# The last batch of the first stage in a three-stage transformer kernel: one POOL operation moved up between its scatters, a table of counts moved behind them, and four experts' weights requested later

## The chip, the cores and the metric

One core of one Trainium2 chip runs the whole program. The engines are PE (matrix products), DVE (vector), ACT (activations), POOL (elementwise sums here, and the issue of indirect transfers), and SP, which only issues transfers. The metric is the device time of one execution in microseconds.

## The reference, cut to what matters

The input is `[8, 512, 256]` in float32. Four layers follow each other, each on the layer-normed stream, each added to it: attention with hyperbolic distances (16 heads of 16), a mixture of experts, attention with a low-rank latent, and a switch-head attention. The change lies where the first layer ends and the experts begin:

```python
logits = x.astype(jnp.float32) @ router_w.T          # 4096 tokens, 64 experts
topk_w, topk_ids = jax.lax.top_k(softmax(logits), K) # K = 8
pos = cumsum(onehot(flat_e), axis=0)[...] - 1        # place of a token among those of its expert
idx = where(pos < C, flat_e * C + pos, E * C)        # C = 128 slots for each of E = 64 experts
xb = zeros(...).at[idx].set(x[tok])                  # a token's row goes to its slots
h = silu(xb @ w_gate) * (xb @ w_up); y = h @ w_down  # w_gate, w_up [256, 192], w_down [192, 256]
routed = segment_sum(y[idx] * weight, tok)
shared = silu(sg) * su @ ws_down                     # two products for every token
```

An expert's weights in float32 are 256 x 384 and 192 x 256 elements, 384 KB and 192 KB (as 128 KB and 64 KB), 576 KB together.

## The kernel before, in words

The kernel has three stages, each a block with a barrier of all engines at its end. Stage one takes the 8 batches (B = 8, 512 tokens each) through the first attention and the routing. Its loop runs over rounds b = -1 to 9, and within each over 8 phases p, one for each pair of heads. Each engine has its own `cycle` function, called once for each (b, p), and the engines meet at semaphores alone. Work that isn't attention is spread over phases by hand-written tables. A batch's routing is done a round after its attention, so round b = 8 has no attention left: only the routing of the last batch, and whatever of the batch before it is open.

A batch's routing ends in a list, slot to token. For batches 0 to 6 POOL writes it: `scatter` issues 32 indirect transfers, each of which writes 128 token numbers of 4 bytes into a table in HBM at slots computed by DVE (`IDX`). In rounds 2 to 7 four of these go into each phase (SCATTERS = 4). Those of batch 6 are all issued in round 8, phase 0, behind the last head sums of batch 7 (`add_root`, L1049). Batch 7's own slots don't go through HBM: DVE makes matrices of marks (`mark`, L884 to L895), PE multiplies them (`list_last`), and DVE adds the result to the list that came back from HBM (`earlier`, L902) into `ids`. The marks need two small tables of counts, which POOL makes with two `iota` (L1074, L1075); a drain and the semaphore `counted` follow, and `mark` waits for it before its first operation.

The chain of the last batch in round 8: the last head group is placed, PE multiplies by `wo` (`output`, two products, each followed by a sum on DVE, L785), DVE takes mean and variance (`stats2`, semaphore `var2`), POOL raises it to the power -0.5 (`rsqrt`, L1042, at phase 4, so behind all that POOL does in phase 0), DVE normalises (`norm2`, L608), PE transposes (`turn2`, L384) and multiplies by the router's weights (`logits`), DVE takes the top 8 (`logits`, `slots`), then gate/up of the shared expert (`gate_up`), the router's weights (`weights`), `hid`, PE's last products and DVE's last sums (`shared`, L942), and SP stores the batch (L319). PE fills idle time with products that nobody reads (`keep_clock`, L365).

SP's order in round 8 is: at phase 3, once all of the attention's products are done, the weights of the first SOON = 4 experts (`request`, three transfers each, L196 to L198); at phase 5 the store of the normalised rows (L327), a wait for all scatters (L331), the load of the list (L332), and the weights of experts 4 to 11 (UN = 12 fit into the buffer); at phase 7 the store of the router's weights (L349); in round 9 the last store of the stream. All of these share one queue; POOL's indirect transfers have their own.

Stage two takes the 64 experts one by one. POOL waits for `ids`, gathers eight experts' rows ahead, then for each expert adds the result to the stream and gathers one more. SP requests expert e's weights when expert e - 12 is done. Stage three is the second attention pair.

## Time and profile before

| | us |
|---|---|
| three timed runs | 2812.64, 2803.64, 2807.13 |
| their median | 2807.13 |
| the profiled execution, its own time | 2811.8 |
| its span in the trace | 2810.1 |

Times in the rows count from the span's start. PE is busy 83% of the span, DVE 68%, ACT 60%, POOL 66%. Stage one lasts to about 1342.5 us, stage two to about 1570. A timeline row gives start, duration, engine, line, operation, output and inputs, and in brackets how long the engine was idle before it and what ended that; "issue" means that the profile shows nothing that it waited for. An engine name with a q is its sequencer, or for SP its queue of transfers.

### The profile page before, as it was taken

What the parts mean: (1) busy time and instruction counts of PE and PEld (TensorE: products, weight loads), DVE (VectorE), ACT (ScalarE), POOL (GpSimd) and SP (SyncE); (2) the same over time, 40 slices, a digit from 0 to 9 for tenths busy, and PEclk for the clock granted to TensorE, in tenths of its full rate; (3) what the DMA queues carried; (4) which work ended last, traced back from release to release, by engine and by line L of the source; (5) the groups of instructions that cost most, each with busy time, mean ns of one, the idle gap of its engine ahead of it and who ended that gap; (6) DMA issues with size and microseconds to landing.
All of it is one profiled execution on the core that took longest, in us unless ns stands there. A gap on an engine that the chain in (4) does not pass through costs nothing. (4 is left out here: it accounts for less than half of the span.)

```text
span 2810.1 us, 31463 instructions
## 1 busy us (share of the span) xinstructions
PE 2339.5 (83%) x10169; PEld 1174.3 (42%) x10169; DVE 1902.4 (68%) x3134; ACT 1673.5 (60%) x2352; POOL 1862.9 (66%) x1858
## 2 busy tenths in 40 slices
PE   5667777787777777775888799999999999999985
PEld 2222323232323323233555455555555555555543
DVE  5787989898988988763333356565756666666655
ACT  1778888889788888980122255555555555555440
POOL 0555587787878787873577302958585858595866
PEclk8667787878778787786899899999999999999997
DMA  3000000000000010114799500000000000000000
GB/s 104 16 1 1 17 16 16 18 16 18 9 25 8 10 23 3 30 15 107 218 265 226 112 1 1 1 1 23 1 23 1 23 1 20 4 8 1 9 0 16
DMA packets 94052, 98.97 MB, mean 35 GB/s; under 512 B 18848, under 2 KB 90656, under 8 KB 93856
## 3 DMA queue, kind: packets, MB, share of 16 engines
q1 hardware_dynamic: 70704, 73.99, 9.1%
q0 software_dynamic: 23152, 22.68, 4.6%
q8 instruction: 84, 1.38, 0.2%
q14 instruction: 112, 0.92, 0.2%
HBM read 69.98 MB, written 26.66 MB: 34 GB/s over the span
## 5 line engine op out<-in xcount | busy, mean ns | idle before, releaser
L1049 POOL TENSOR_TENSOR TT<-TT,SS 128x512 f32<-128x512 f32 x512 | 652.0, 1309 | 223.8 <-ACT SS L978 223.3
L1791 ACT ACTIVATE PR<-S,NM 128x512 f32<-128x512 f32 x512 | 345.3, 686 | 260.2 <-DVE NM L1958 260.2
L1958 DVE TENSOR_REDUCE NM<-S 128x2 f32<-128x1024 f32 x256 | 301.7, 1220 | 131.7 <-PE S L1685 131.7
L734 DVE TENSOR_SCALAR TT<-SC 128x1024 f32<-128x1024 f32 x256 | 311.6, 1217 | 75.4 <-POOL TT L1049 44.6
L464 PE MATMUL OB<-TT,VAL 128*17 128x512 f32 x1024 | 345.3, 777 | 4.6 <-ACT TT L986 4.6
L736 DVE SCALAR_TENSOR_TENSOR SS<-SC,TT 128x1024 f32<-128x1024 f32 x256 | 313.6, 1225 | 20.6 <-issue 1.8
L1054 POOL DMA_INDIRECT slot_tokens<-TID,IDX x224 | 229.3, 1024 | 101.1 <-issue 67.1
L1696 PE MATMUL TP<-ident,PR 128*128 128x128 f32 x2048 | 273.3, 276 | 21.2 <-DVE TT L1963 18.2
L1696 PEld LDWEIGHTS TP<-ident,PR 128*128 128x128 f32 x2048 | 235.0, 142 | 113.7 <-issue 66.9
L1963 DVE COPY TT<-TP 128x512 f32<-128x512 f32 x256 | 176.3, 689 | 151.4 <-PE TP L1696 147.6
L1797 ACT ACTIVATE TT<-TP 128x512 f32<-128x512 f32 x256 | 153.3, 599 | 195.1 <-PE TP L1696 191.3
L1715 PE MATMUL OT<-TT,VN 128*64 128x512 f32 x1024 | 251.4, 612 | 14.7 <-POOL VN L2055 14.7
L1685 PE MATMUL S<-TT 64*128 64x512 f32 x1024 | 257.5, 621 | 0.7 <-ACT TT L1760 0.7
L986 ACT ACTIVATE TT<-TT 128x2048 f32<-128x2048 f32 x128 | 244.6, 1911 | 9.7 <-issue 0.4
L982 ACT ACTIVATE TT<-TT 128x2048 f32<-128x2048 f32 x128 | 243.4, 1901 | 0.2
L978 ACT ACTIVATE SS<-SS 128x2048 f32<-128x2048 f32 x128 | 240.4, 1904 | 0.7
L443 PE MATMUL SC<-QT,KT 54*128 54x512 f32 x512 | 156.4, 609 | 94.0 <-DVE SS L736 90.6
L2055 POOL TENSOR_TENSOR VN<-VN,VM 128x256 f32<-128x256 f32 x256 | 187.4, 732 | 36.7 <-issue 0.4
L443 PEld LDWEIGHTS SC<-QT,KT 54*128 54x128 f32 x512 | 57.6, 222 | 292.8 <-DVE SS L736 214.1
L2051 POOL TENSOR_TENSOR VN<-XV,WV 128x256 f32<-128x256 f32 x64 | 40.1, 626 | 193.8 <-DVE WV L1953 193.8
L2051 POOL TENSOR_TENSOR VM<-XV,WV 128x256 f32<-128x256 f32 x256 | 160.1, 625 | 9.1
L2088 POOL TENSOR_TENSOR GT<-AH,MO 128x320 f32<-128x320 f32 x196 | 136.0, 725 | 28.4 <-issue 26.9
(293 smaller groups left out, 4083.9 us busy)
## 6 DMA issues: line engine op xcount, KB each, us to landing
TT<-w_gu SPq DMA_DIRECT2D x64, 384.0 KB
TT<-w_dn SPq DMA_DIRECT2D x64, 128.0 KB
XL<-x SPq DMA_DIRECT2D x8, 512.0 KB
stream<-V SPq DMA_DIRECT2D x4, 1024.0 KB, 10.3
rows<-XL SPq DMA_DIRECT2D x8, 512.0 KB
TT<-w_dn SPq DMA_DIRECT2D x64, 64.0 KB
XS<-stream SPq DMA_DIRECT2D x8, 512.0 KB, 4.3
out<-XS SPq DMA_DIRECT2D x8, 512.0 KB, 2.9
```

Of the source, the lines that this page charges most:

```text
L464: ins = pe.matmul(OB[r:r + DH0 + 1, :], values_of[:, mt, h, :], TT[:, h % RING, mt, :], start=(mt == 0), stop=(mt == NT - 1))
L734: dve.tensor_scalar(tt[:, :, mt, :], SC[mt % 2][:], 0.0, None, ALU.max)
L736: dve.scalar_tensor_tensor(ss[:, :, mt, :], SC[mt % 2][:], 2.0, tt[:, :, mt, :], ALU.add, ALU.mult)\
L978: act.activation(half(SS, GH, h), half(SS, GH, h), ACT.Sqrt).then_inc(sems["root"], 1)
L982: act.activation(half(TT, RING, h), half(TT, RING, h), ACT.Ln, bias=1.0)
L986: act.activation(half(TT, RING, h), half(TT, RING, h), ACT.Exp, scale=-1.0).then_inc(sems["p"], 1)
L1049: ins = pool.tensor_tensor(tt, tt, ss, ALU.add)
L1685: ins = pe.matmul(S[s % 2][:, h2, :], QT[r % 2][lo:lo + DH1, pair, j * P:(j + 1) * P], KT[r % 2][lo:lo + DH1, 0 if kind == 1 else pair, :] ...
L1696: ins = pe.transpose(TP[h2][:, m * P:(m + 1) * P], PR[s % 2][h2][:, m * P:(m + 1) * P], ident[:])
L1715: ins = pe.matmul(OT[lo:lo + DH1, :], VN[r % 2][:, m, h * DH1:(h + 1) * DH1], PT[pair % 2][h2][:, m, :], start=(m == 0), stop=(m == NT - 1))
L1791: act.activation(PR[s % 2][h2][:], S[s % 2][:, h2, :], ACT.Exp, bias=NM[:, s % 2, h2:h2 + 1], accum_out=SM[:, pair % 2, j, h2:h2 + 1]).the ...
L1958: dve.tensor_reduce(NM[:, s % 2, :], S[s % 2][:], AX, ALU.max, negate=True).then_inc(sems["peak"], 1)
```

## The change

POOL, round 8: of the 32 scatters of batch 6, the first 20 (AHEAD = 5 x 4) stay in phase 0. In phase 4 comes the power of the last batch's variance, and then the other 12 scatters, and then the two iotas with their drain and the semaphore `counted`, which stood in front of all scatters. SP, round 8: SOON is 0, so no expert's weights are requested at phase 3; the wait there stays. All 12 experts' weights are requested at phase 5, behind the load of the slot list. What is computed is the same.

```diff
 CLEARS = 4
+AHEAD = 5 * SCATTERS
...
-SOON = 4
+SOON = 0
...
                 if p == 4 and before:
                     rsqrt(v, 1, "var2", "rstd2")
-                if p == 0 and b == B:
+                if p == 4 and b == B:
+                    for c0 in range(AHEAD, NT * K, SCATTERS):
+                        scatter_of(v, c0)
                     pool.iota(count_i, [[1, P]], base=0, channel_multiplier=0)
                     pool.iota(own.bitcast(I32), [[0, 1]], base=0, channel_multiplier=1)
                     pool.drain()
                     pool.sem_inc(sems["counted"], 1)
                 if p == 0 and b == B:
-                    for c0 in range(0, NT * K, SCATTERS):
+                    for c0 in range(0, AHEAD, SCATTERS):
                         scatter_of(v, c0)
```

## Rows read from the trace of the kernel before

**Rows 1.** Busy time by stretch: end of stage one, stage two.
```profile
core 0: us, PE busy (x) PEld busy (x) DVE busy (x) ACT busy (x) POOL busy (x), PEclk, DMA share, GB/s
1245.00:1342.50 97.50, 57.81 (x209) 30.61 (x205) 33.94 (x93) 16.24 (x15) 32.37 (x35) 0.71 0.42 91
1342.50:1570.00 227.50, 194.57 (x808) 128.57 (x808) 74.94 (x192) 45.67 (x128) 164.57 (x128) 0.97 0.87 223
```

**Rows 2.** Waits, 1240 to 1400: total us, times, longest; DVE's, then SP's.
```profile
DVE XL L608 <- POOL rstd L1042: 18.2, 1, 18.2
...
SPq L331 <- DMA slot_tokens<-TID,IDX: 4.2, 2, 3.7
```

**Rows 3.** Timeline of POOL: second iota, first and last scatter, power, first gather.
```profile
1245.12 0.14 POOL L1075 IOTA AM<- 128x1 int32 x1
1252.88 1.00 POOL L1054 DMA_INDIRECT slot_tokens<-TID,IDX  x1 [7.62 <-issue]
...
1292.41 0.97 POOL L1054 DMA_INDIRECT slot_tokens<-TID,IDX  x1 [0.30 <-issue]
1293.40 1.04 POOL L1042 TENSOR_TENSOR rstd<-var,mhalf 128x4 f32<-128x4 f32 x1
...
1343.33 1.04 POOL L1129 DMA_INDIRECT XG<-rows,ids  x1 [48.89 <-POOLq L300]
```

**Rows 4.** Timeline, behind a drain of POOL: at the start, and in stage three.
```profile
5.34 0.23 DVE L2238 CAST selq<-selw 128x128 fp32r<-128x128 f32 x1 [5.34 <-POOLq L2232]
...
1964.70 2.77 POOL L2088 TENSOR_TENSOR GT<-AH,MO 128x320 f32<-128x320 f32 x4 [5.34 <-issue]
```

**Rows 5.** Timeline of PE: two sets of transposes, and `output`.
```profile
1261.12 0.66 PE L384 MATMUL WKA<-ident,AO 128*128 128x128 f32 x4 [0.25 <-issue]
...
1262.46 3.72 PE L390 MATMUL WKD<-wo,XT 128*128 128x256 f32 x16 [0.25 <-issue]
...
1295.99 1.12 PE L384 MATMUL WKA<-ident,XL 128*128 128x128 f32 x4 [24.65 <-issue]
```

**Rows 6.** Timeline of DVE: second output sum, variance, marks, list, last sum.
```profile
1273.44 0.69 DVE L785 TENSOR_TENSOR QK<-QK,WKD 128x512 f32<-128x512 f32 x1 [7.15 <-remote]
...
1276.16 0.17 DVE L603 TENSOR_SCALAR var<-mv 128x4 f32<-128x4 f32 x1
...
1315.17 0.22 DVE L884 CAST RR<-NR 128x128 f32<-128x128 int32 x1
...
1323.35 0.21 DVE L902 CAST ST<-TT 64x128 f32<-64x128 uint32 x1
...
1338.45 0.69 DVE L942 TENSOR_TENSOR QK<-QK,WKD 128x512 f32<-128x512 f32 x1 [3.91 <-PE WKD L554]
```

**Rows 7.** Timeline of SP's issues: list, first and last of eight experts' weights.
```profile
1300.66 0.46 SPq L332 DMA_DIRECT2D TT<-slot_tokens  x1
1301.53 0.38 SPq L196 DMA_DIRECT2D TT<-w_gu  x1
...
1314.88 0.47 SPq L198 DMA_DIRECT2D TT<-w_dn  x1
```

**Rows 8.** Transfers issued, 1300 to 1342: KB each, us to landing.
```profile
stream<-QK SPq DMA_DIRECT2D x1, 512.0 KB, 2.9
rows<-PW SPq DMA_DIRECT2D x1, 128.0 KB, 2.0
TT<-slot_tokens SPq DMA_DIRECT2D x1, 32.0 KB, 3.5
```

**Rows 9.** Busy time by stretch: four early experts, idle PE, eight experts.
```profile
1257.00:1279.00 22.00, 12.80 (x48) 7.30 (x46) 7.52 (x18) 1.19 (x2) 16.82 (x18) 0.89 0.82 108
1274.00:1296.00 22.00, 0.01 (x1) 0.01 (x1) 3.47 (x14) 0.00 (x0) 15.86 (x17) 0.51 0.16 31
1303.00:1318.00 15.00, 13.62 (x46) 7.06 (x45) 10.95 (x42) 1.70 (x2) 0.00 (x0) 0.82 0.96 290
```

**Rows 10.** Timeline, batch 7: a normalisation on DVE, a scatter beside it.
```profile
1183.05 1.53 DVE L608 TENSOR_SCALAR XL<-X,mv,rstd 128x256 f32<-128x256 f32 x4
1183.14 1.03 POOL L1054 DMA_INDIRECT slot_tokens<-TID,IDX  x1 [0.20 <-issue]
```

## The prediction

> **What bounds the kernel now.** I read the table by stage first, because a change to one batch must be judged in its own stretch. In the stretch from 1245 to 1342.5 us no engine is near busy: PE works 57.8 us of 97.5, DVE 33.9, POOL 32.4 [rows 1]. So a chain of waits sets this stretch, not an engine's load. The next stage, the 64 experts, keeps POOL busy 164.6 us of 227.5 with its gathers and adds, which follow each other without a break; it starts when the last batch is done and keeps its length, so what is won before 1342.5 us moves the end one for one.
>
> The waits then say where the chain stands still: DVE's normalisation (L608) waited 18.2 us for `rstd`, which POOL computes, and SP waited for the scatters in front of the slot list (L331) [rows 2]. POOL's timeline shows why: 32 scatters in a row, the power only behind them, ending at 1294.44 [rows 3]. DVE had the variance ready at 1276.33 [rows 6]. From the power on, the chain runs norm, transposes, logits, top 8, slots, marks, hidden product, last sum at 1339.14, store, landing 2.9 us later [rows 6, 8]. That landing is what the stage's end waits for: the store is issued right behind the sum, at 1339.2, and 1339.2 + 2.9 = 1342.1; POOL's first gather leaves at 1343.33, released by the barrier [rows 3]. I take 1342.1 as the end to be moved.
>
> **POOL's order.** The first scatter started 7.62 us behind the two iotas, while its slots (released by DVE long before, as the row gives no releaser but "issue") were there [rows 3]. In that gap stand a drain and a semaphore. A drain behind iotas with no transfer issued before it costs nothing: DVE is released at 5.34 [rows 4]. In stage three, with one transfer of POOL's own (the merge of a batch) issued in front of it, the work behind the next drain started 5.34 us late [rows 4]. So I give the gap to the drain, 7.62 less the 0.30 that every scatter waits: 7.3 us, bounds 0 and 7.6. It moves with the iotas behind the last scatter.
>
> - First scatter: directly behind the sum at 1245.1, where the iota began [rows 3]. Pace: (1292.41 - 1252.88) / 31 = 1.275 us. Twenty take 25.5: done at 1270.6.
> - The power then needs the variance. Before, the second output product's sum on DVE started 7.15 us after its engine was free, released by something that the trace calls remote, though PE's products ended at 1266.18 (1262.46 + 3.72) [rows 5, 6]. That wait lies inside the stretch in which the four early experts moved at 108 GB/s beside the scatters, against 290 GB/s for the eight without them [rows 9]. With those requests gone I take the wait as gone: the sum starts at 1266.3 and the variance, which came 1276.33 - 1273.44 = 2.9 us after it, at 1269.2. Bounds: 1269.2 to 1276.3.
> - Power: 1270.6 + 1.04 gives `rstd` at 1271.7 instead of 1294.4, a shift of **22.7 us**.
> - PE's clock: it fell to 0.51 in the idle stretch before the transposes [rows 9]. Now PE's last filler ends near 1271.3 and work returns at 1273.3, so I expect 1.00 there. Two sets of transposes then take 0.66 instead of 1.12 each [rows 5]: 0.9 us more.
> - Marks: DVE's first step of them (L884) ran at 1315.17 [rows 6] and would be ready at 1315.17 - 22.7 - 0.9 = 1291.6. It now waits for the counts: twelve scatters behind the power, 12 x 1.275 = 15.3, to 1287.2; iotas 0.3 and drain 7.3: 1294.8. Queued behind that wait on DVE are two gate/up copies, the router's weights, the hidden product and both last sums, so all of the tail gets the smaller shift, 1315.17 - 1294.8 = 20.4. Last sum: 1339.14 - 20.4 = 1318.8.
>
> **A rule against this order.** The moved scatters run beside DVE's normalisation, SBUF to SBUF in float32. In batch 7 the same pair met, and the scatter took 1.03 us beside a norm of 1.53 [rows 10], against 0.96 to 0.97 elsewhere: 0.07 us, which I leave out of the sum. The Trainium skill, "SBUF — State Buffer", section on the two separate sides, says that a DVE instruction in a two-port mode locks POOL out of writing descriptors until it ends. By that rule the norm would cost its whole length, 1.5 us, on the counts and the list; by the row nothing.
>
> **SP's order.** Removed: 12 issues (4 experts) from 1257 on. They move behind the slot list, so the list is followed by 36 issues in place of 24. The list was issued at 1300.66, 7.3 us after the last scatter's end at 1293.38 [rows 3, 7]. Now: 1287.2 + 7.3 = 1294.5; requests from 1295.4. The list lands 3.5 us after its issue in rows 8, at 1298; DVE needs it behind the second marks, 1323.35 - 20.4 = 1303 [rows 6], so it costs nothing (were it over 4 us later, it would be next). An expert's three issues take (1314.88 + 0.47 - 1301.53) / 8 = 1.73 us [rows 7]; twelve take 20.7, to 1316.1. Behind them on SP is the store of the router's weights (ready near 1300, so it waits 16 us, nobody for it but the barrier) and then the last store, wanted at 1318.8: SP is free in time. The queue is not. Twelve experts are 12 x 576 KB = 7.08 MB; at the 290 GB/s of the eight [rows 9] that is 24.4 us, and 1.0 for the first data: done at 1320.8. Behind it on the same queue come the 128 KB of router weights, 1.1 us (its landing of 2.0 less about 0.9 of latency), and the last 512 KB, 1.6 us of data and about 1.0 to land (of its 2.9) [rows 8]: **1324.5**. Without the queue it would be 1318.9 + 2.9 = 1321.8. So the gain is the smaller one, 1342.1 - 1324.5 = **17.6 us**; the counts' lateness is hidden by the queue.
>
> All twelve experts are there when the next stage starts, as before, so it finds the same state. Sum against the profiled execution: 2811.8 - 17.6 = 2794.2 us (its span 2810.1 becomes 2792.5). That execution lies 4.7 above the median of the three timed runs, 2807.13, so the forecast is 2807.1 - 17.6 = **2789.5 us**. The three runs lie 9 us apart.
>
> **The rivals.**
> - *The queue does not hold the last store.* If the scatters landed about 2 us after issue, list and experts would go 5.3 us earlier, the queue would be empty at 1316.6, and the store would land at 1321.8: gain 20.3, 2787 us. For it: the queue's end and the store's issue are 3.1 us apart in my sum. Against: 7.3 us in rows 3 and 7. If the drain cost nothing too, the last sum would be at 1315.6 and the landing near 1319.2: 22.9 us, 2784. The Trainium skill, "DMA: Bandwidth & Descriptors", section on the anatomy of a POOL transfer, gives about 2.0 us fixed for issue to completion, which is this rival; the trace differs from it here.
> - *DVE's 7 us wait stays.* Variance at 1276.33, power at 1277.5, twelve scatters to 1292.9, list at 1300.2, experts done at 1326.5, last store landed at 1330.2: gain 11.9, 2795 us. For it: its releaser is not named. Against: it falls exactly beside the removed transfers.
> - *The gap is not the drain's*, so the change does not do what it says for POOL: scatters from 1252.9, twenty to 1278.4, `rstd` at 1279.5, the rest to 1294.9, list at 1302.2, experts done at 1328.5, landing 1332.2: gain 9.9, 2797 us. Against: rows 4.
> - *Something unseen eats over half of it*, in the expert stage or in the clock's fall and rise: gain under 8.4, the bound named below.
> - *Slower: twelve experts at the slow rate.* Four experts beside scatters ran at 108 GB/s [rows 9]. If that rate held for all twelve, 7.08 MB would take 65.6 us, to 1361, and the last store, behind them on the queue, would land at 1365: 23 us later than now, 2830 us. It decides from about 170 GB/s down (7.7 MB in the 45 us between 1296 and 1341). Against: SP waits for all scatters before the first request, and eight experts behind that same wait ran at 290.
>
> **How the numbers follow.** Main case 0.57, with its own range 2785 to 2794 (the queue's end within 1.5 us, the median's scatter of some 3). No hold by the queue 0.12; DVE's wait stays 0.12; gap stays 0.05; unseen loss 0.09; slower 0.05. The range reaches from 2783 (22.9 us and a little scatter) to 2798 (9.9 us and a little scatter) and leaves 2 in 10 outside. Within 0.3%, 8.4 us, a measurement of this kernel can hardly tell a change from none. Faster by more: the first four cases, 0.86; within: 0.09; slower: 0.05.
>
> **What the profile after would show.** First scatter near 1245 with no 7 us gap in front; twenty, then a power near 1271; a gap of 5 to 8 us behind the iotas, of which DVE's L884 waits some 3 us; DVE's second output sum with no remote wait; PE's clock 1.00 at the transposes; list near 1294.5; transfers near 290 GB/s without a break to 1321; the last store landing 5 to 6 us after its issue, not 2.9; first gather near 1325; the expert stage and all behind it as long as before. I am wrong if the variance comes after 1271, if the scatters slow down beside the 512 KB store of the normalised rows, which now runs among them, or if the first gather comes at 1335 or later.

## The result, and the profile after

The median is 2802.84 us in 20 runs (2792.69 to 2809.78), against 2806.78 in 20 runs of the kernel before made beside them (2800.73 to 2812.64). The ratio is 0.9985, with a 95% interval of 0.9978 to 0.9991: the change is worth 4.2 us (2.5 to 6.2), within the 0.3% that the prediction called no change. It forecast 17.6. The profiled execution took 2800.45 us, its span 2798.7.

The first view is POOL's timeline of the kernel after (start, duration, operation, idle before it and its releaser). Line numbers are one higher than before, three higher in stage two.

```profile
1245.51 0.98 POOL L1055 DMA_INDIRECT slot_tokens<-TID,IDX  x1
...
1269.54 0.96 POOL L1055 DMA_INDIRECT slot_tokens<-TID,IDX  x1 [0.30 <-issue]
1277.02 1.04 POOL L1043 TENSOR_TENSOR rstd<-var,mhalf 128x4 f32<-128x4 f32 x1 [6.53 <-DVE var L604]
1278.26 1.03 POOL L1055 DMA_INDIRECT slot_tokens<-TID,IDX  x1 [0.20 <-issue]
...
1296.40 0.96 POOL L1055 DMA_INDIRECT slot_tokens<-TID,IDX  x1 [4.46 <-issue]
1297.37 0.25 POOL L1077 IOTA NR<- 128x128 int32 x1
1297.57 0.16 POOL L1078 IOTA AM<- 128x1 int32 x1
1335.45 1.00 POOL L1132 DMA_INDIRECT XG<-rows,ids  x1 [37.73 <-POOLq L301]
```

The gap of 7.62 us ahead of the first scatter [rows 3] is gone, and 20 scatters are through at 1270.5, as forecast. Then two things stand here that no row of before showed. POOL has nothing to do for 6.5 us, because the variance is late, and ahead of the very last scatter it stops for 4.46 us. The first gather comes at 1335.45; it was at 1343.33, and 1325.7 was forecast.

DVE's timeline of the kernel after, the lines that answer to [rows 6]:

```profile
1273.45 1.28 DVE L786 TENSOR_TENSOR QK<-QK,WKD 128x512 f32<-128x512 f32 x2 [9.97 <-remote]
...
1276.76 0.17 DVE L604 TENSOR_SCALAR var<-mv 128x4 f32<-128x4 f32 x1
...
1293.80 0.42 DVE L827 TENSOR_TENSOR LG<-WKD,CNT 128x256 f32<-128x256 f32 x1 [3.96 <-remote]
...
1305.53 0.23 DVE L885 CAST RR<-NR 128x128 f32<-128x128 int32 x1 [5.11 <-POOLq L1079]
...
1313.70 0.21 DVE L903 CAST ST<-TT 64x128 f32<-64x128 uint32 x1
...
1328.81 0.69 DVE L943 TENSOR_TENSOR QK<-QK,WKD 128x512 f32<-128x512 f32 x1 [3.91 <-PE WKD L555]
```

The wait called remote is there still, and there is a second one at L827, the slots' sum. The marks (L885) wait 5.11 us for the counts. What stands between the transposes and the first of these sums is in ACT's and PE's timelines of the kernel after:

```profile
1260.85 0.60 ACT L991 ACTIVATE XT<-WKA 128x512 f32<-128x512 f32 x1 [5.19 <-issue]
1264.91 0.60 ACT L991 ACTIVATE XT<-WKA 128x512 f32<-128x512 f32 x1 [3.46 <-remote]
```

```profile
1261.51 0.66 PE L385 MATMUL WKA<-ident,AO 128*128 128x128 f32 x4 [0.25 <-issue]
...
1265.57 5.41 PE L391 MATMUL WKD<-wo,XT 128*128 128x256 f32 x16 [2.97 <-issue]
```

PE's second set of transposes ends at 1262.17, and ACT, idle and waiting for exactly them, starts at 1264.91: 2.7 us late. The 16 products then take 5.41 us, not 3.72 [rows 5], and end at 1270.98, and DVE starts on them at 1273.45, another 2.5 us late. In each case PE has finished by the profile and the engine that waits for it is not let go. I call this a late release. The ends of PE's work are modelled in this profile, so it doesn't exclude that PE itself ended later than shown.

The slots' sum (L827) shows when it comes to an end. Its products end at 1290.84, the row of 11 scatters on POOL ends at 1291.94, and the sum starts at 1293.80. In eight more profiles below (e2, e5, e6, e8, e14 to e17) it also starts 1.9 to 2.2 us behind the end of the unbroken row beside it, though its products ended 4.8 to 7.8 us before it. Where no release is late (e11, e12 and e19, for instance) it starts 0.1 us behind its products, while the row still runs or after it.

SP's issues and the transfers of the kernel after, answering to [rows 7, 8]:

```profile
1305.30 0.47 SPq L333 DMA_DIRECT2D TT<-slot_tokens  x1
...
1326.23 0.47 SPq L199 DMA_DIRECT2D TT<-w_dn  x1
1326.81 0.52 SPq L350 DMA_DIRECT2D rows<-PW  x1
1329.57 0.37 SPq L320 DMA_DIRECT2D stream<-QK  x1
```

The list is issued 7.9 us behind the last scatter's end. From the last store to the first gather there are now 5.9 us (1329.57 to 1335.45) in place of 4.1 (1339.21 to 1343.33): the store is held on its queue.

The busy times by stretch of the kernel after. The first two lines are its end of stage one and its stage two, the third its norm's transposes and logits, the fourth its twelve experts:

```profile
1245.00:1335.00 90.00, 58.84 (x204) 31.70 (x205) 34.08 (x93) 16.63 (x15) 32.54 (x36) 0.75 0.38 99
1335.00:1565.00 230.00, 192.36 (x810) 127.79 (x810) 74.89 (x192) 45.53 (x128) 164.17 (x130) 0.98 0.87 220
...
1279.00:1287.00 8.00, 7.08 (x29) 5.85 (x30) 1.09 (x3) 1.19 (x2) 6.04 (x7) 0.60 0.27 66
1306.00:1330.00 24.00, 14.65 (x54) 8.53 (x55) 15.14 (x30) 2.04 (x3) 0.00 (x0) 0.54 1.00 283
```

The work is the same as in [rows 1]; only the waits differ. The experts run at 283 GB/s without a break, and the granted clock at the norm's transposes is 0.60, not 1.00.

The clock also costs time at the end of the chain, from the addition of the list (L903) to the start of the last sum. The same stretch in the kernel after, and in its second profile (e14 below):

```profile
1313.70:1328.81 15.11, 13.46 (x43) 7.34 (x44) 7.42 (x17) 1.19 (x2) 0.00 (x0) 0.50 1.09 303
1320.86:1331.33 10.47, 8.82 (x43) 5.42 (x44) 7.43 (x16) 1.19 (x2) 0.00 (x0) 0.82 1.08 312
```

At the lower of the two clock levels (0.50) it takes 15.1 us, as it did before (1323.35 to 1338.45), and at 0.82 it takes 10.5. The sum of the prediction carried the 15.1 us over without a word.

### The profile page after: what moved, and what is told of

Same layout as the page of the kernel before. It is cut to its first block and busy times, and to the rows that moved or that the text cites. A ratio compares the mean times of both kernels' runs of the same rounds, so it can differ in the third digit from the quotient of the medians.

```text
span 2798.7 us, 31464 instructions
## 1 busy us (share of the span) xinstructions
PE 2334.1 (83%) x10169; PEld 1175.5 (42%) x10169; DVE 1903.8 (68%) x3134; ACT 1672.3 (60%) x2352; POOL 1861.2 (67%) x1858
## 5 line engine op out<-in xcount | busy, mean ns | idle before, releaser
L465 PE MATMUL OB<-TT,VAL 128*17 128x512 f32 x1024 | 338.9, 764 | 7.9 <-ACT TT L987 7.9
```

Source lines behind the costliest of these rows:

```text
L465: ins = pe.matmul(OB[r:r + DH0 + 1, :], values_of[:, mt, h, :], TT[:, h % RING, mt, :], start=(mt == 0), stop=(mt == NT - 1))
```

## The experiments

Eighteen runs were made, in five groups; three of them (e14, e16, e19) repeat the kernel after, e11 and e17. The kernels of a group ran on one chip beside runs of the kernel before, and each group on another chip; I call these A to E. No chip was used twice, so a difference between chips can't be told from one between the times of the groups. Which chip the kernel after was first measured on is not on record. Where one execution alone was made, its time is given without an interval, and the profile counts.

### Chip A: the parts apart

The kernel before took 2806.83 us here (median of 23).

**e1, the weights alone** (the kernel before, without the early requests):

```
-SOON = 4
+SOON = 0
```

> The kernel before with SOON = 0 alone. Theory S (PE's releases come late while POOL's scatters are in flight, whatever else moves): DVE's second output sum still waits some 7 to 10 us and starts near 1273, the power still ends near 1294 behind 32 scatters, the last store still lands near 1342: no change in time, within 2 us of before. Theory W (the early experts' transfers made that wait, as the forecast took it): the sum starts near 1266, but the power is behind the scatters all the same: no change in time either. What tells them apart is the start of that sum.

Measured: 2801.82 us, ratio 0.9985 (0.9974 to 0.9996). One row of DVE's waits (total us, times, longest):

```profile
DVE QK L785 <- remote: 3.7, 1, 3.7
```

The wait of 7.15 us is smaller, 3.7, but not gone, and the gap ahead of the first scatter is 7.62 us as before. The wait costs nothing here, since POOL is late anyway; what the kernel gains is behind the power, where the clock rises sooner (from `rstd` to the marks 17.6 us, before 20.7).

**e2, POOL's order alone** (the kernel after, with the early requests):

```
-SOON = 0
+SOON = 4
```

> POOL's new order alone, with four experts requested at phase 3 as before. If the new order alone brings the gain: power near 1278, list near 1305, last sum near 1329.5, and since only 8 experts stand in front of the last store it lands 2.9 us after its issue, near 1332.5: 1 to 2 us faster than the changed kernel, about 6 us faster than before. If the early requests slow the scatters down, as the forecast's slower rival has it for the rate of both: power 1279 or later, list 1308 or later, no gain over the changed kernel.

Measured: 2802.32 us, ratio 0.9978 (0.9969 to 0.9987). The waits of DVE:

```profile
DVE QK L786 <- PE WKD L391: 17.1, 2, 14.9
...
DVE LG L827 <- remote: 6.2, 1, 6.2
```

The wait at the output sums is 14.9 us, 10.0 in the kernel after, and `rstd` comes at 1285.3. But the last store, with eight experts ahead of it, is followed by the first gather in 4.1 us, not 5.9. So twelve experts behind the list cost the store 1.8 us, and the parts don't add: 0.9985 and 0.9978 apart, 0.9985 together.

**e3, no scatters in the last batch.** This kernel leaves out the last round's 32 scatters, so the slot list lacks the tokens of one batch, and SP doesn't wait for them; all else is the kernel after.

```
-                        sp.wait_ge(sems[f"scattered{i}"], 16 * NT * K // LANES * (B - 1))
+                        sp.wait_ge(sems[f"scattered{i}"], 16 * NT * K // LANES * (B - 2))
...
-                    for c0 in range(AHEAD, NT * K, SCATTERS):
-                        scatter_of(v, c0)
...
-                    for c0 in range(0, AHEAD, SCATTERS):
-                        scatter_of(v, c0)
```

> The changed kernel without the 32 scatters of round 8 (batch 6's slots stay empty in the list). Theory S: no remote wait on DVE, second output sum near 1266.5, variance near 1269.5, power near 1270.6; no late release at the slots' product; counts at once behind the power (drain 5 to 7 us: marks near 1291). List issued near 1273. Theory P (something of PE itself, its code or its fillers, which is at the same place in all these kernels): the sum still starts near 1273 and the variance comes at 1276 to 1277.

Measured: 2781.51 us in one execution. Of DVE's waits:

```profile
DVE QK L786 <- PE WKD L391: 2.4, 2, 1.5
```

DVE waits 2.4 us in all at the output sums, and no wait of its or ACT's is called remote. Its second output sum is at 1267.5, `rstd` is there at 1271.5, the marks start at 1287.9 and the last store at 1311.9. PE's work at this place is as before, so it isn't PE itself; the weights aren't requested yet either.

This kernel also shows what a drain costs when no transfer is in flight. Its last one was issued at 1218.03, and the drain behind the iotas, in the sequencer's record (xcount: duration in ns, start), is

```profile
L1077 POOLq DRAIN  x1: 8152/8152/8152, 1270.4 to 1270.4; - x1
```

It ends at 1278.55, 6.8 us behind the end of the second iota (1271.76). In the kernel before it ends 6.8 us behind the iota too (1252.04), 34 us after the last scatter was issued. So the drain's 7 us are not the time that transfers in flight need.

**e4, the power first** (all 32 scatters behind it):

```
-AHEAD = 5 * SCATTERS
+AHEAD = 0
```

> The changed kernel with AHEAD = 0: all 32 scatters behind the power. Theory S: nothing of POOL's is in flight when PE makes the output, so the second sum starts near 1266.5 and the power ends near 1270.6; then 32 scatters to 1312 or later, list near 1319, counts near 1320, last store landing near 1350: 8 us slower than before. PE's releases behind the power are late again by 2 us or more while scatters run. Theory P: power near 1278 and everything 7 us later still.

Measured: 2822.15 us in one execution. DVE's waits:

```profile
DVE GU L815 <- remote: 20.8, 2, 18.6
DVE LG L827 <- remote: 7.6, 1, 7.6
```

Up to the power nothing is late (`rstd` at 1271.2). Behind it, where the row of scatters now stands, DVE waits 7.6 and 18.6 us for releases of PE, with no weights moving; for the second of these PE's products had ended at 1292.5 and DVE starts at 1312.3. The late releases follow the scatters. With e1 and e3 this shows, for chip A, that the wait which the prediction took from the early requests is one of PE's late releases beside POOL's row of scatters. Whether the requests add to it isn't shown: it is smaller in e1, which has none, but in e14 below, which has none either, it is as long as in e2.

### Chip B: the counts, the drain, the pace, the kind

The kernel before took 2809.39 us here, in one execution.

**e5, the counts in the idle stretch** (iotas, drain and release between the 20th scatter and the power):

```
                 if p == 4 and b == B:
+                    pool.iota(...); pool.iota(...); pool.drain()
+                    pool.sem_inc(sems["counted"], 1)
+                if p == 4 and before:
+                    rsqrt(v, 1, "var2", "rstd2")
+                if p == 4 and b == B:
                     for c0 in range(AHEAD, NT * K, SCATTERS):
```

> The changed kernel with one move: POOL's two count ramps, its drain and the release stand behind the first 20 scatters and in front of the power, in the 6.5 us in which POOL is idle there. Drain theory: a drain costs about 7.5 us wherever POOL's own transfers stand ahead of it, so POOL is ready for the power at 1270.5 + 0.4 + 7.5 = 1278.4, the power is some 1 to 2 us later than the 1277.0 of the changed kernel; the marks' wait (5.1 us, VectorE on POOL) is gone, and the list is requested 7.9 us behind the last scatter's end. Theory that the 4.5 us stop ahead of the 32nd scatter comes from a long row of transfers without a drain between them: the stop is gone here, the last scatter ends near 1294 and the list is requested near 1302 (1305.3 in the changed kernel). Rival for the stop, that it belongs to the 32nd transfer or to its place in time: the stop of 4 to 5 us stays and the list is requested at 1306. Rival for the drain, that it costs only what is still in flight and so about 1 us on top of the idle time: then the power is at 1277.0 as before.

Measured: 2802.93 us in one execution. POOL's timeline, from the second iota:

```profile
1269.90 0.16 POOL L1074 IOTA AM<- 128x1 int32 x1
1283.02 1.04 POOL L1043 TENSOR_TENSOR rstd<-var,mhalf 128x4 f32<-128x4 f32 x1 [12.95 <-DVE var L604]
...
1298.33 0.96 POOL L1055 DMA_INDIRECT slot_tokens<-TID,IDX  x1 [0.30 <-issue]
```

The drain now costs nothing, but only because the variance is later still: the drain ends at 1280.6 and the power starts at 1283.02. With the variance of the forecast it would have held the power back by some 10 us. Beyond that, the marks no longer wait, and the stop ahead of the last scatter is gone. So the stop goes with a drain in front, as one theory said. The gain is eaten by releases that are later here than in the kernel after.

**e6, no drain** (each iota releases DVE itself):

```
-                    pool.drain()
-                    pool.sem_inc(sems["counted"], 1)
+                    (both iotas with .then_inc(sems["counted"], 1); DVE waits for 2)
```

> The changed kernel without POOL's drain behind the two count ramps: each ramp releases VectorE itself. Drain theory: the 7.7 us between the ramps (1297.6) and VectorE's first mark (1305.5) shrink to under 1 us, so the first mark starts when its own predecessor ends (about 1300.4, since its wait for POOL was 5.1 us), and everything behind it up to the last store comes 4 to 5 us earlier unless the list, requested at 1305.3 and landed some 3.5 us later, is late next: then the gain is only 1 to 3 us and a wait for the list stands ahead of the last step of the marks' chain. Rival, that it is the transfers themselves and not the drain that hold POOL's releases back: the first mark still starts at 1304 or later.

Measured: 2805.75 us in one execution. Timelines of POOL, of DVE and of SP's issues:

```profile
1303.77 0.97 POOL L1055 DMA_INDIRECT slot_tokens<-TID,IDX  x1 [4.87 <-issue]
...
1304.95 0.16 POOL L1078 IOTA AM<- 128x1 int32 x1
```

```profile
1307.31 0.22 DVE L885 CAST RR<-NR 128x128 f32<-128x128 int32 x1
...
1326.12 0.69 DVE L943 TENSOR_TENSOR QK<-QK,WKD 128x512 f32<-128x512 f32 x1 [1.82 <-PE WKD L555]
```

```profile
1334.42 0.51 SPq L320 DMA_DIRECT2D stream<-QK  x1
```

The marks start behind DVE's own work, 2.2 us after the second iota's end and with no wait for POOL. The 7.7 us of before are the drain's. The stop stays. And a third limit shows: the last sum is done at 1326.81, but SP issues the last store at 1334.42, since the list was late (1312.2) and 37 issues stand between. Where DVE is in time, the last store comes 22.2 us behind the list, by SP's issues alone.

**e8, the scatters spread** (behind each of the first 20, POOL writes 384 integers to a tile that is free):

```
+                    room = SS[:].rearrange("p h m n -> p (h m n)").bitcast(I32)
+                    pool.iota(room[:, 384 * c:384 * (c + 1)], [[1, 384]], base=0, channel_multiplier=0)
```

> The changed kernel with a write of 384 integers by POOL behind each of the first 20 scatters, so that a scatter is issued about every 2 us in place of every 1.26 us; the written tile holds nothing that is still needed. The power comes late by construction (POOL reaches it at 1286 or later), so only VectorE's waits are read. Theory that TensorE's releases are held back by the rate at which POOL issues scatters: VectorE's wait of 10 us for a release of TensorE at 1273.5 shrinks to under 3 us. Rival, that a transfer in flight from POOL's queue is enough at any pace: VectorE still starts that operation at 1273 or later, behind a wait of 7 us or more, and the attention output's products are late too. A third case, that only POOL's own work on the SBUF port matters, would make the wait longer than in the changed kernel, since POOL is busy with its writes as well.

Measured: 2800.67 us in one execution. ACT's two copies:

```profile
1259.73 0.60 ACT L991 ACTIVATE XT<-WKA 128x512 f32<-128x512 f32 x1 [5.18 <-PE WKA L385]
1261.07 0.60 ACT L991 ACTIVATE XT<-WKA 128x512 f32<-128x512 f32 x1 [0.74 <-PE WKA L385]
```

At 1.65 us a scatter neither these nor the output sums' release is late (second sum at 1265.5, DVE's two waits there 2.4 us together), on the chip on which e5 and e6, at 1.26 us, had waits of 13.2 and 14.4 us at L786. POOL is slower by construction and reaches the power at 1277.7, and still this kernel is no slower than e5 and e6. The second row of this same kernel, 11 scatters at the full pace behind the power, ends at 1292.62, and there a release is late: the slots' products end at 1289.90 and their sum starts at 1294.70. So within one execution the slow row shows no late release and the fast one does. By this profile the pace matters, and not that a transfer is in flight.

**e9, plain transfers** in place of the last round's indirect ones (same queue, 128 elements of 4 bytes each, to consecutive rows, so the list holds other tokens):

```
-                    pool.indirect_dma_start(table, bass.IndirectOffsetOnAxis(ap=IDX[:, c:c + 1], axis=0), ...
+                    pool.dma_start(table[c * P:(c + 1) * P, :], TID[:, c // K:c // K + 1])...
```

> The changed kernel with the 32 indirect scatters of the last round replaced by 32 plain transfers from the same queue of POOL with the same 128 elements of 4 bytes, to consecutive rows of the slot table (the list then holds other tokens in other slots, and the output is another one; the work is the same). Theory that any row of POOL-queued transfers holds TensorE's releases back: VectorE's operation at 1273.5 still waits 7 us or more and the stop of 4 to 5 us ahead of the last one stays. Rival, that it is the indirect kind (descriptors that POOL computes from the indices): no wait over 1 us for TensorE's releases, as without scatters, power at 1271.5, no stop ahead of the last transfer.

Measured: 2792.64 us in one execution. POOL's timeline:

```profile
1247.07 10.70 POOL L1058 DMA_DIRECT2D slot_tokens<-TID  x20
...
1291.60 0.54 POOL L1058 DMA_DIRECT2D slot_tokens<-TID  x1 [10.35 <-issue]
```

No release is remote, but this doesn't settle the kind: a plain one takes POOL 0.54 us, so the row was over at 1257.8, ahead of the transposes that suffer. What it settles is the stop: it is there for plain transfers too, 10.35 us and again ahead of the 32nd. That transfer is also the 224th into this table since the kernel's start; no run tells the two counts apart.

### Chip C: more ahead, and a drain where POOL is idle

**e7, 24 scatters ahead of the power** (`AHEAD = 6 * SCATTERS`).

> The changed kernel with 24 scatters in front of the power in place of 20. Theory that TensorE's releases come only when the back-to-back row of scatters has thinned out: the row ends at 1275.8, and VectorE's wait for TensorE ends after that (1277 to 1285; 1273.5 behind 20 scatters in the changed kernel, 1277.5 to 1279.3 in two later kernels with 20), so the power is at 1280 or later and POOL is idle 4 us or more. Rival, a delay that belongs to the place in time and not to the row: VectorE goes on at 1273.5 to 1279 as with 20, and the power follows at once. In both the stop of 4 to 5 us ahead of the 32nd scatter stays.

**e11, an early drain** in POOL's idle 7.5 us at 1228, and the iotas as in e6 but between the 20th scatter and the power:

```
                 if p == PAIRS - 1 and 1 <= b < B - 1:
                     scatter_of(v, 0)
+                if p == PAIRS - 1 and b == B - 1:
+                    pool.drain()
```

> The changed kernel with POOL's drain moved into its idle 7.5 us at 1228 (nothing of it in flight there) and the two count ramps between the 20th scatter and the power, each releasing VectorE itself. Theory that the stop ahead of the last scatter comes from a row of transfers without any drain between them, wherever the drain stands: the 8 x 28 + 32 transfers are cut at 1228 and the stop of 4 to 5 us is gone, so the last scatter ends 12 x 1.26 us behind the power (some 15.4) and the list is requested 7.9 us later. Drain theory: a drain with nothing in flight costs under 1 us and VectorE waits for POOL neither at the marks nor before. Rival: the stop belongs to the 32nd scatter and stays; or the drain at 1228 takes 5 to 7 us and its end pushes the last additions (from 1235.5) back.

**e12, joined**: e11 with 24 scatters ahead and the last four experts' requests behind the last store.

> The kernel with the early drain, with 24 scatters in front of the power and the last four experts' twelve requests moved behind the last store. By the theory of late releases the power is at 1280 to 1284, the last 8 scatters end at 1291 to 1294 with no stop, the list is requested at 1299 to 1302 and the marks start at about 1298, so the last store is at 1322 to 1325 (list plus 22 us) and the first gather 4.1 us behind it in place of 5.9, at 1327 to 1330: 5 to 8 us before the changed kernel's 1335.5, median 2795 to 2798. If the list's and the marks' paths were not what sets the last store, it stays at 1329 and the median at 2801 to 2803.

**e13, joined and spread**: e11 with the spread row and the requests of e12.

> The kernel with the early drain, with a write of 384 integers behind each of the first 20 scatters (one every 1.65 us, so TensorE's releases come in time) and the last four experts' requests behind the last store. Theory: the power is at 1278 whatever the run, the last scatter ends at 1294, the list is requested at 1302, the marks start at 1296, the last store is at 1324 and the gather at 1328: median 2796 to 2799, as good as the joined kernel without the writes or a little worse in the list. If the releases' lateness is only a matter of luck between runs and not of the pace, VectorE's wait of 7 us or more for TensorE shows up here too.

Measured: e7 2795.06 and e11 2780.90 us in one execution each, beside 2801.36 for the kernel before; e12 2793.18, ratio 0.9973 (0.9961 to 0.9985); e13 2797.32, ratio 0.9984 (0.9975 to 0.9992). None of the four shows a late release at the output sums, e7 neither, which has no early drain. POOL in e11:

```profile
1269.79 0.17 POOL L1074 IOTA AM<- 128x1 int32 x1
1269.89 1.05 POOL L1043 TENSOR_TENSOR rstd<-var,mhalf 128x4 f32<-128x4 f32 x1
...
1324.05 1.00 POOL L1133 DMA_INDIRECT XG<-rows,ids  x1 [37.98 <-POOLq L301]
```

This is the forecast's own course: 20 scatters, the power at once, `rstd` at 1270.9. There is no stop in e11 to e13, and one of 6.04 us in e7. The early drain of e11 is

```profile
L1088 POOLq DRAIN  x1: 15129/15129/15129, 1218.8 to 1218.8; - x1
```

It ends at 1233.9, 6.8 us behind POOL's work before it (1227.14) and 10.7 us ahead of the row. The additions behind it start on ACT's release at 1234.61, as before. So it isn't free: its 6.8 us fit into an idle stretch of 7.5. In e12 and e13 the first gather is 8.9 us behind the last store, for SP must first issue twelve requests: a worse place than the one they came from. And 24 ahead put `rstd` at 1275.5, four scatters later than e11's.

### Chip D: is it the drain, the execution or the chip?

**e14** is the kernel after once more, **e15** is it with the early drain alone, **e16** is e11 again, and **e17** is e11 with the last four experts requested at the start of stage two:

```
-                    for e in range(SOON, UN):
+                    for e in range(SOON, UN - 4):
...
         def _(sp):
+            for e in range(UN - 4, UN):
+                request(sp, sems, (w_gu, w_dn), into, e)
             for dst, src in early:
```

> The changed kernel once more, as the control of its neighbours. If lateness is a matter of the execution or of the schedule without an early drain, VectorE waits 7 us or more for TensorE ahead of the last attention output's addition in most such profiles, this one included (five of seven so far), and the median is about 0.15% under the kernel before. If it belongs to the chip, the wait is absent wherever it is absent in the neighbours. The stop of 4 to 5 us ahead of the 32nd scatter is there in any case.

> The changed kernel with one more drain of POOL in its idle 7.5 us at 1228 and nothing else. Stop theory: the 4.5 us stop ahead of the last scatter is gone. Theory that the early drain also rids the scatters of what holds TensorE's releases: no wait over 3 us for TensorE in VectorE's rows, power at 1271, last scatter's end at 1286, list at 1294, marks held by the count's drain until 1294; last store at about 1318, first gather at 1325, median 8 to 14 us under that of the changed kernel beside it. Rival, lateness by the execution: only the stop's 4.5 us go, the median is 2 to 5 us under the changed kernel's.

> The kernel of e11 again, now timed. If the 2780.9 us of its single run holds, the median is 2780 to 2786, some 20 us under the kernel before: power at 1271, list at 1293, store at 1316, gather at 1324, stage two and three at 455 us together. If that run was a lucky one (its stages two and three were 7 to 14 us shorter than other profiles show), the median is 2788 to 2793.

> The kernel of e11 with the last four experts' twelve requests issued at the start of stage two, behind the barrier and not ahead of it. Theory: of the 8.3 us between the last store and the first gather in e11, 4 to 5 are the queue's hold by the weights; with eight experts requested the store lands in about 3 us and the gather is 4.1 us behind the store, median 3 to 5 us under e11's. Rival, that stage two pays it back, since the weights of the ninth expert then come later: stage two is longer by as much and the median is the same.

Measured, beside 2808.95 for the kernel before: e14 2803.76, ratio 0.9987 (0.9978 to 0.9996); e15 2800.35, 0.9973 (0.9962 to 0.9984); e16 2801.63, 0.9969 (0.9959 to 0.9979); e17 2798.26, 0.9963 (0.9951 to 0.9976). All four profiles have late releases. ACT in e16, the same kernel as e11:

```profile
1266.43 0.60 ACT L991 ACTIVATE XT<-WKA 128x512 f32<-128x512 f32 x1 [9.71 <-remote]
1274.89 0.60 ACT L991 ACTIVATE XT<-WKA 128x512 f32<-128x512 f32 x1 [7.86 <-remote]
```

and PE beside it:

```profile
1261.22 0.66 PE L385 MATMUL WKA<-ident,AO 128*128 128x128 f32 x4 [0.23 <-issue]
...
1267.09 1.11 PE L385 MATMUL WKA<-ident,AO 128*128 128x128 f32 x4 [4.78 <-issue]
...
1275.55 6.73 PE L391 MATMUL WKD<-wo,XT 128*128 128x256 f32 x16 [6.49 <-ACT XT L991]
```

The first transposes end at 1261.88 and ACT starts 4.6 us later; the second end at 1268.20 and ACT starts 6.7 us later; then the products run at the lower clock, 6.73 us in place of 3.72. In e11 the same copies stood at 1259.96 and 1261.31. So the early drain doesn't decide, and an execution's luck is unlikely to: four profiles of four kernels without late releases on one chip, four of four with them on another, and one of the kernels is the same on both. The chip, or the time of the group, is what is left. The stop is another matter: it is gone in e15, e16 and e17 and there (5.43 us) in e14. The drain that removes it is the one thing in which e15 (0.9973) differs from e14 (0.9987). By the medians that is 3.4 us, with intervals that overlap. The four later experts bring the gather back to 4.1 us behind the store (e16 has 6.9), and end SP's queue of issues sooner.

### Chip E: the best version again

**e18** is e17 with the spread row, **e19** is e17 again.

> The kernel with the early drain and the last four experts' requests in stage two, with a write of 384 integers by POOL behind each of the first 20 scatters, so that one is issued every 1.65 us in place of 1.26. Pace theory: no wait over 3 us of VectorE or ScalarE for TensorE up to the power even where the control beside it has them; POOL itself is last, so the power is at 1279 (1245 + 20 x 1.65 + 1), the last scatter ends at 1295, the list is requested at 1303, the last store is at 1324 and the gather at 1328, some 8 us before the control's if that one has late releases: median 5 to 9 us under it. Rival, that the chip decides and the pace does nothing: where the control has late releases this one has them too and is no faster.

> The control of the spread row, the kernel of e17 again: on a chip with late releases the power is at 1283 to 1286 and the last store at 1331 to 1333; on a chip without them the power is at 1271, the last store at 1316, the gather at 1320 and the median about 2790.

Measured, beside 2802.97 for the kernel before: e18 2786.84, ratio 0.9942 (0.9929 to 0.9956); e19 **2781.83**, ratio 0.9918 (0.9904 to 0.9931). In neither is a release late. The control itself had none, so the pace could not be put to the test here; it showed only what spreading costs where nothing is late, 5.0 us. POOL and SP in e19:

```profile
1271.30 1.04 POOL L1043 TENSOR_TENSOR rstd<-var,mhalf 128x4 f32<-128x4 f32 x1
...
1318.69 1.00 POOL L1135 DMA_INDIRECT XG<-rows,ids  x1 [30.86 <-POOLq L301]
```

```profile
1295.34 0.47 SPq L333 DMA_DIRECT2D TT<-slot_tokens  x1
...
1314.58 0.37 SPq L320 DMA_DIRECT2D stream<-QK  x1
```

e17 and e19 are one kernel on two chips: `rstd` at 1284.2 and 1272.3, first gather at 1336.6 and 1318.7, ratios 0.9963 and 0.9918. On each chip its executions agree (2796.81 to 2801.79 us in six, 2778.75 to 2782.16 in five), so this isn't a matter of single executions. The kernel before is faster too on the chips where no release was late (2801.36 and 2802.97 us on C and E, 2806.83 to 2809.39 on the others); it wasn't profiled there.

## Why the prediction was wrong, step by step

**The step that failed** is the one that reads "With those requests gone I take the wait as gone". It put the variance at 1269.2; it was there at 1276.93, and `rstd` at 1278.06 in place of 1271.7, 6.4 us late. The wait lay beside the early transfers, but it also lay beside the scatters, and the change brought those closer to it: they now run from 1245.5 on, over PE's transposes and output products. e3 and e4 show that the late releases go where the row of scatters goes, and in e1, without the requests, 3.7 of the 7.15 us are still there. What the requests add isn't shown. The second bound of that step, 1276.3, was near the truth, and the prediction gave that rival 0.12 for the wrong reason: a wait that has no name in a trace should be set against every transfer that runs beside it, POOL's own included.

**What followed from it.** The marks were forecast at 1294.8 and started at 1305.53, 10.7 us late. Of that 6.4 are the power's, and 4.2 are the stop ahead of the last scatter (4.46 less the usual 0.30), a term that the prediction didn't have: the pace of 1.275 us did not contain it and no row of before showed it. It stands where no drain comes between the rounds before and the last transfer (after, e2, e4, e6 to e9, e14), and not where one does (before, e1, e5, e11 to e13, e15 to e19). The drain that the change moved away had been preventing it; by what mechanism is open. So the rival "DVE's wait stays", 11.9 us, was also too good: with the stop it would be 7.7, and the profiled execution won 7.9 at the first gather.

**Why the median won only 4.2** is shown in part. The lateness differs between the two profiles of the kernel after: in the second, e14, `rstd` came at 1284.9 and the first gather at 1342.3, 1.0 us before that of the kernel before and not 7.9. But what lies behind the first gather differs as much: it took 1466.8 us in the profile of the kernel before, 1463.3 in the first of the kernel after and 1456.6 in e14, whose execution was the fastest of its eleven (2800.66 us) in spite of its late gather. From the first gather to the start of stage three alone the profiles of this study lie between 222.7 and 229.5 us. So of the 11.4 us between the two profiled executions only 7.9 lie where the change is, and a single execution can't be set against the medians.

**PE's clock** was forecast at 1.00 at the transposes and was 0.60: the late variance left PE idle for 3.6 us ahead of them. From `rstd` to the logits it took 8.5 us (9.8 before, 6.3 in e3, where the clock stayed up), so about 2 us went there.

**What held.** The gap of 7.62 us was the drain's: it went away with the iotas, and stood again behind the last scatter (1297.73 to 1305.53, 7.8 us; 7.3 forecast), and e6 without a drain has 2.2. The prediction gave the drain this price because transfers had been issued in front of it. That they were in flight isn't the reason, since e3 shows 6.8 us some 50 us behind POOL's last transfer, while the first drain of stage three takes 0.4 us in the kernel before; what sets its length is open. The scatters' start (1245.5; 1245.1), their pace (20 done at 1270.5; 1270.6), the list 7.9 us behind them (7.3), the requests' 20.9 us on SP (20.7), and the queue at 283 GB/s (290). The queue does hold the last store, by 1.8 us where 2.7 were forecast, and e2 and e17, with eight experts ahead of it, don't show that hold. That SP itself was free in time held in the first profile of the changed kernel (1327.3, two us ahead of the last sum's end) and not in its second, e14: there the last sum is done at 1332.02 and SP issues the store at 1335.05. The rival in which the queue does not hold the last store needed a landing about 2 us behind the issue. That is the fixed time of a POOL transfer that the Trainium skill gives in "DMA: Bandwidth & Descriptors", section on the anatomy of a DMA; the list is issued 6.6 to 7.9 us behind the last scatter's end in these kernels, so the rival fell. Against the norm, 128 x 256 on DVE, a scatter took 1.03 us as in [rows 10]. The Trainium skill, "SBUF — State Buffer", section on the two separate sides, says that a DVE instruction in a two-port mode keeps the shared ports until it ends and POOL waits. No such wait shows here, and no run shows whether the norm is in such a mode. Its row of 1.53 us is four instructions, so the prediction's price of the whole 1.5 us took them for one. Stage two kept its length within the spread named above (229.2 us; 227.3).

**Where the forecast's course is real.** On chips C and E, where no release came late, e11 and e19 ran it: the power right behind 20 scatters, `rstd` at 1270.9 and 1272.3 against 1271.7 forecast. Those two also have no stop and no drain behind the scatters, so they don't show that the change as forecast would have won 17.6 us. The changed kernel itself was not run on such a chip; e7, nearest to it there, was 6.3 us under the kernel before in one execution.

**What stays open.** Why PE's releases come late on three chips and not on two isn't known, nor whether it is the chip at all or something of the time of the group. That a slower pace avoids it rests on one profile, e8, which has both paces in it, on a chip whose two other kernels with all indirect transfers at full pace had it. Whether it needs indirect transfers was not settled by e9. And since PE's ends are modelled, it isn't shown whether the release is late or PE itself.

## What to carry to other kernels

A long row of small transfers issued by POOL is not free for the others: ask who waits for PE beside it, and keep the row away from a chain of short PE steps. A drain may be worth more than it costs; before moving one, look which transfers it stands between, and put it into an idle stretch that is longer than the drain. And a gain of under 1% that hangs on such overlaps should be timed on more than one chip: the best version here was worth 0.4% on one and 0.8% on another.

## What the runs showed of the hardware

- PE's releases reached ACT or DVE 2.5 to 19.8 us after the end of PE's work, by the profile, while POOL issued scatters of 128 x 4 bytes every 1.26 to 1.28 us (chips A, B, D, and the two profiled executions of the result); not at 1.65 us (e8, B), not without scatters (e3, A), and not at all on chips C and E. The slots' sum came 1.9 to 2.2 us behind the end of the row in nine profiles.
- Ahead of the 32nd transfer of a last round, the 224th in all, without a drain since the rounds before POOL stopped for 4.2 to 6.0 us (10.35 with plain transfers); one drain removed it, even one that ended 10.7 us ahead of the round.
- A drain of POOL behind its scatters or its additions in stage one ended 6.4 to 8.2 us behind POOL's last work (10.6 in e5), also where no transfer had been issued for 50 us (6.8, e3). It cost nothing only where POOL was idle for longer than that. The first drain of stage three took 0.4 us.
- The last 15.1 us of the chain, at a granted clock of 0.50, took 10.5 us at 0.82.
